# Marking the rows of a bucketed edge sum: three DVE comparisons with a scalar and two ACT operations become one DVE comparison of two tensors

## The reference, cut to what matters

```python
edge_index = jnp.stack([src, dst])
# x: 6250 x 128, edge features: 206250 x 128
row = edge_index[0]                                   # = src, unsorted node numbers
edge_aggr = zeros((n, 128)).at[row].add(edge_features)
combined = concatenate([x, edge_aggr, global_expand], -1) @ W_c + b_c
h = softplus(combined @ W1 + b1)
h = softplus(h @ W2 + b2)
out = layernorm(x + (h @ W3 + b3))
```

## Time and profile before

| | us |
|---|---|
| median of 3 runs | 2045.82 |
| their lowest and highest | 2043.21, 2053.67 |
| the profiled execution's own time | 2045.75 |
| its span, from the first to the last instruction | 2043.8 |

### The profile page before, as it was taken

How to read it: one execution, slowest core, us unless ns; L and a number is a source line. 1 busy time by engine, 2 the same in 40 slices (tenths; PEclk the granted TensorE clock), 3 DMA queues, 4 the chain that set the end, 5 groups by cost and what they waited for, 6 DMA issues and landing times.

```text
span 2043.8 us, 61008 instructions
## 1 busy us (share of the span) xinstructions
PE 1837.2 (90%) x14853; PEld 1709.6 (84%) x14853; DVE 1309.8 (64%) x3881; ACT 1038.7 (51%) x3479; POOL 1170.9 (57%) x1482
## 2 busy tenths in 40 slices
PE   7888988898898989998998889898988999999986
PEld 4788888888888888887888888788888999999973
DVE  7755555555555555555565555555656998899866
ACT  1443443343444444444443444344446888888886
POOL 1656656656655655665665665565564555555535
PEclk9899988898899999899999898999998999999998
DMA  5488666666656665665565556565657999999942
GB/s 139 156 265 277 198 207 207 202 191 211 207 180 173 174 173 166 175 183 165 172 187 173 172 161 184 163 180 161 186 174 222 299 304 300 296 298 305 304 138 61
DMA packets 166150, 413.19 MB, mean 202 GB/s; under 512 B 28533, under 2 KB 43813, under 8 KB 163896
## 3 DMA queue, kind: packets, MB, share of 16 engines
q1 hardware_dynamic: 103824, 234.69, 38.1%
q0 software_dynamic: 54608, 174.58, 27.5%
q10 hardware_dynamic: 7689, 3.60, 1.0%
HBM read 234.52 MB, written 178.23 MB: 202 GB/s over the span
## 4 chain that ended last, share of the span: by engine, by line
PE 77%; issue 8%; DVE 5%; another core or an unknown queue 3%; POOL 1%; ACT 1%; POOLq 1%; DMA 1%; DVEq 0%; ACTq 0%; SPq 0%
PE ps L1228 51%; PE ps L1300 19%; PE ps L1199 2%; PE ps L1186 2%; DVE arena L803 2%; PE ps L1190 1%; DVE hotc L641 1%; DVE arena L875 1%; PE ps L1335 1%; PE ps L1196 1%; DVE slot_f L660 0%; POOL sums L564 0%; DVE picked L652 0%; POOLq L559 0%
## 5 line engine op out<-in xcount | busy, mean ns | idle before, releaser
L1228 PE MATMUL ps<-arena 128*120 128x129 f32 x9084 | 1229.3, 291 | 98.6 <-issue 87.7
L1228 PEld LDWEIGHTS ps<-arena 128*120 128x120 f32 x9084 | 1141.5, 193 | 130.8 <-issue 117.3
L522 POOL DMA_INDIRECT buckets<-arena,index x757 | 778.8, 1029 | 549.2 <-ACT arena L1013 341.3
L803 DVE TENSOR_SCALAR arena<-slot_no,slot_f 128x360 f32<-128x360 f16 x1514 | 549.1, 415 | 601.3 <-PE ps L1228 332.7
L1013 ACT ACTIVATE arena<-ps 120x387 f32<-120x387 f32 x757 | 372.6, 493 | 851.8 <-PE ps L1228 519.5
L1300 PE MATMUL ps<-mark,members 128*128 128x128 f32 x3648 | 412.7, 276 | 9.0 <-ACT mark L1114 7.1
L1300 PEld LDWEIGHTS ps<-mark,members 128*128 128x128 f32 x3648 | 410.5, 192 | 11.2 <-issue 10.4
L847 DVE TENSOR_SCALAR mark<-node_no,members 128x128 f32<-128x128 f16 x1368 | 360.7, 330 | 55.1 <-DMA members<-buckets 45.9
L564 POOL TENSOR_TENSOR sums<-sums,staged 128x128 f32 x456 | 226.4, 496 | 197.5 <-ACT staged L1102 119.5
L968 ACT ACTIVATE reach<-block_no,arena 128x120 f16<-128x120 f16 x806 | 313.4, 391 | 0.7 <-PE ps L1238 0.7
L1108 ACT ACTIVATE apart<-node_no,members 128x128 f32<-128x128 f16 x456 | 181.0, 397 | 34.3 <-DMA members<-buckets 26.6
(11 more groups left out here) (169 smaller groups left out, 634.6 us busy)
## 6 DMA issues: line engine op xcount, KB each, us to landing
members<-buckets SPq DMA_DIRECT2D x456, 258.0 KB, 3.6
arena<-in_feats SPq DMA_DIRECT2D x201, 516.0 KB
buckets<-arena,index POOLq DMA_INDIRECT x757
xn<-in_x ACTq DMA_DIRECT2D x1, 2800.0 KB
arena<-in_xT SPq DMA_DIRECT2D x11, 250.0 KB, 3.9
out_rows<-xn SPq DMA_DIRECT2D x11, 224.0 KB
buckets<-arena,direct_at POOLq DMA_INDIRECT x98
arena<-in_src SPq DMA_DIRECT2D x1, 805.5 KB
```

The lines of the kernel that those rows point to most:

```text
L522: pool.indirect_dma_start(units, bass.IndirectOffsetOnAxis(ap=index[0:SLOTS, s, b:b + 1], axis=0), rows[0:SLOTS, o, :], None).then_inc(sca ...
L803: dve.tensor_scalar(perm[0:TP, b, t, :], slot_no[0:TP, :, :].rearrange("p r b -> p (r b)"), slot_f[0:TP, s, b * TPB + t:b * TPB + t + 1], ...
L1228: mm = pe.matmul(ps[0:SLOTS, MOVED + b, r * ROWF:(r + 1) * ROWF], perm[0:TP, b, t, r * SLOTS:(r + 1) * SLOTS], feat[0:TP, s, b * TPB + t, ...
```

## The change

The four marks of a step are made by one `tensor_tensor` on DVE. Its first input is `node_no` repeated four times, its second the four node numbers of the partition, each repeated 128 times; 512 columns come out. ACT's two operations for the fourth mark, their tile `apart` and the semaphores `apart_made` and `last_marked` are gone. ACT's part of the second phase is the evictions alone, and TensorE waits for `marked` only. Everything else stays as it is.

```diff
             def mark_nodes(s, m, turn):
+
                 dve.wait_ge(members_loaded[m], turn * 16 + 16)
                 wait(dve, summed, s - 3)
-                for r in range(QR - 1):
-                    last = dve.tensor_scalar(mark[:, m % 4, r, :], node_no[:, :],
-                                             members[:, m, r * ROWF + D:(r + 1) * ROWF], None, ALU.is_equal)
-                last.then_inc(marked, 1)
+                ids = members[:, m, :].rearrange("p (r f) -> p r f", f=ROWF)[:, :, D:ROWF]
+                dve.tensor_tensor(mark[:, m % 4, :, :], node_no[:, :].unsqueeze(1).to_broadcast([P, QR, P]),
+                                  ids.to_broadcast([P, QR, P]), ALU.is_equal).then_inc(marked, 1)
...
-            def last_apart(s, m, turn):
-                act.wait_ge(members_loaded[m], turn * 16 + 16)
-                wait(act, last_marked, s - 1)
-                act.activation(apart[:, m % 2, :], node_no[:, :], ACT.Abs, scale=-1.0,
-                               bias=members[:, m, QR * ROWF - 1:QR * ROWF]).then_inc(apart_made, 1)
-
-            def last_mark(s, m):
-                act.wait_ge(apart_made, s + 1)
-                wait(act, summed, s - 3)
-                act.activation(mark[:, m % 4, QR - 1, :], apart[:, m % 2, :], ACT.Relu, scale=-1.0, bias=1.0)\
-                   .then_inc(last_marked, 1)
-
-            def act_step(s, m, turn):
-                ends = isinstance(s, int)
-                if not ends or s + 3 < STEPS:
-                    last_apart(s + 3, (m + 3) % MS, turn + (m + 3) // MS)
-                if not ends or s + 2 < STEPS:
-                    last_mark(s + 2, (m + 2) % MS)
-                evict_sums(s, m)
...
             for m in range(MS):
-                act_step(m, m, 0)
-            with act.Fori(1, STEPS // MS - 1) as i:
+                evict_sums(m, m)
+            with act.Fori(1, STEPS // MS) as i:
                 for m in range(MS):
-                    act_step(i * MS + m, m, i)
-            for m in range(MS):
-                act_step(STEPS - MS + m, m, STEPS // MS - 1)
+                    evict_sums(i * MS + m, m)
...
             def sum_members(s, m):
                 pe.wait_ge(marked, s + 1)
-                pe.wait_ge(last_marked, s + 1)
                 wait(pe, evicted, s + 1 - MS)
```

More of the change, by code:

```diff
@@ L183, in gnn_bucketed_edge_sum_mlp_layernorm @@
         staged = sb("staged", [P, 4, P])
-        apart = sb("apart", [P, 2, P])
         wc = sb("wc", [P, 3, D])
@@ L304, in gnn_bucketed_edge_sum_mlp_layernorm @@
         marked = sem("marked")
-        apart_made = sem("apart_made")
-        last_marked = sem("last_marked")
         summed = sem("summed")
```

## The result

The changed kernel takes 2065.61 us (median of 6 runs) against 2045.59 for the kernel before (6 runs beside them): the ratio is 1.0096, with a 95% interval of 1.0073 to 1.0118, so 15 to 24 us slower. 2059 had been forecast, with 2044 to 2083 as the range. The profiled execution has a span of 2064.0 us against 2043.8.

What follows compares the result with a forecast made beforehand. POOL's instruction stream was taken as the bound, not TensorE. From 2045.75 us, 0.8 gained from evictions and 14.3 lost where DVE and POOL exclude each other gave +13.5, so 2059 us, range 2044 to 2083.

Steps and rivals of the forecast that it cites:

- The bound: Second phase: POOL's instruction stream, 7.26 us a turn, sets the end; TensorE is 0.1 us a turn faster.
- The cost of the comparison: DVE: the one comparison of 512 columns takes 0.69 us, hidden under TensorE's 0.90 us a step.
- Exclusion, and from which point: DVE and POOL: held-off adds end 0.31 us after DVE, held-off comparisons 0.55 after POOL; together 0.86 us a step.
- The sum: POOL's turns in the second phase: 0.25 us lost a turn, 14.3 us over 57 turns, bounds 0 and 44.
- one miss of 0.57 us in three turns: POOL's loop end: an add comes late and waits through a DVE comparison, 0.19 us a turn.
- The term for `b3`: DVE's addition of `b3` after its mark, in 50 of 57 turns, delays POOL: 0.06 us a turn.
- The 0.8 us to be gained from evictions: End of the second phase: POOL waits less because ACT's evictions stand behind nothing, 0.8 us saved, at most 1.1.
- The longest adds: Sign in POOL's adds: mean of 0.55 to 0.65 us instead of 0.496, some above 1.0.
- The wait at the end: Sign at L1321, start of the third phase: TensorE's wait for POOL grows from 2.23 us towards 10.
- Slack: Rival: POOL's slack takes it all and its turn stays 7.26 us; 2045 us, not slower; chance 0.29.
- DVE goes twice before a waiting POOL: Rival: POOL waits through two DVE operations, one more miss of 0.57 us a turn; 2092 us, chance 0.17.
- Full blocking: Rival: DVE and POOL exclude each other for whole instructions, 1.14 us a step; 2151 us, chance 0.02.

Runs made afterwards that it cites:

- the PSUM kernel: Changed kernel with the comparison's node numbers read from PSUM, one input left in SBUF, and sums on four banks instead of eight: 2046.80 us, ratio 1.0007.
- the two kernels with 24 steps: 24 steps instead of 8 in POOL's loop body: in the changed kernel 2049.61 us, ratio 1.0019; in the kernel before 2044.42 us, ratio 0.9987.

## Why the prediction was right

- *The bound.* POOL's instruction stream sets the end, not TensorE's 99.9% busy: shown by the PSUM kernel, where TensorE was faster and the end was not, and by the two kernels with 24 steps, where an edit of POOL's loop alone moved the chain. Reading starts instead of durations was what found it.
- *The cost of the comparison.* 0.69 us forecast; 0.68 to 0.69 where nothing disturbs it, and 0.691 with an input in PSUM. Right.
- *Exclusion, and from which point.* The figure of the earlier trace rows, 0.31 us, holds throughout the changed kernel: all 337 adds of over 0.50 us end 0.30 to 0.33 after an operation of DVE with two inputs in SBUF. The 0.55 us worked out from the earlier trace rows holds too: the 297 comparisons of over 0.72 us that an add held off end 0.55 after it (median; 0.546 to 0.552 for nine in ten). Right.
- *The sum.* 14.3 us for POOL's turns; the chains of two profiles of each kernel differ by 15.3 on average (430.7 against 415.4). That it comes so near is in part luck, for its split was wrong. I had one miss of 0.57 us in three turns, 19 in all, and a slack of 0.12 us from an add of 0.57 that kept its pace. The slack reaches further, to adds of 0.67, so that the longest add of the changed kernel, 0.996, costs 0.33. But there are 99 misses, in 47 of the 57 turns, of 0.17 us in the mean, and only 24 of them are the first add behind a loop's end. Fewer misses of a higher price and more of a lower one gave nearly the same sum. The term for `b3`, 3.4 us, lies inside the 1 to 4 that the runs allow. The 0.8 us to be gained from evictions didn't come: the chain of the PSUM kernel, where they stand behind nothing on ACT either, is 415.0.
- *The rest of the 20 us.* Between the first profiles of both kernels the spans differ by 20.2 us: 16.1 in the chain, 2.2 behind it, where the clock was low in one and not in the other, and 1.9 ahead of it, in the first phase, whose starts scatter by more than that. The forecast had nothing for the last two.
- *The longest adds.* Some above 1.0 were forecast; the longest is 0.996, and 1.014 in the second profile.
- *The wait at the end* was forecast at the first product with `sums`. It came a line earlier, at the product with x, which waits for the evictions: 5.96 + 1.87 us instead of 10.
- *Rivals.* Slack does not take it all: it takes the median add, 0.645, but not the 99 above 0.67. That DVE goes twice before a waiting POOL never happened in the changed kernel: in its trace no add waits through two of DVE's operations, and the longest, 0.996, began when a comparison of 0.69 had just begun (0.69 + 0.31 = 1.00). What the earlier trace rows show is an addition that follows a comparison with a scalar; a comparison of two tensors behind another let POOL in each time. Full blocking would have made 1.14 us a step; the chain has 431.0 / 456 = 0.95.

## What to carry to other kernels

An engine with 57% busy time can be the bound: take the distance between the starts of its instructions and compare it with that of the engine that looks full, before crediting anything to the latter. When an operation gets a second tensor input in SBUF, look at what POOL does beside it, add up how long both hold the other off in one step, and if it comes near the step's length, try one input in PSUM: here that cost banks but no time, and took the whole loss back. Cutting the operation into two shorter pieces gained nothing here, because their sum no longer fitted.

## What the runs showed of the hardware that I had not expected

TensorE's granted clock fell during the wait at the end of the second phase, and stayed low for a while even under load. A stretch of the changed kernel:

```profile
1985.70:1995.90 10.20, 6.42 (x11) 3.44 (x12) 0.48 (x1) 2.54 (x7) 2.72 (x6) 0.50 0.00 0
```

TensorE had made nothing since 1981.66. Its clock was still at 1.00, the 2.4 GHz level, up to 1985.6, and at 0.50, the 1.2 GHz level, from 1985.7 to 1995.9, although it had work again from 1987.62 on. Where it was kept busy with spare products the clock stayed at 1.00. The length of the wait alone doesn't say whether the clock falls. In the first profile of the kernel before it stayed at 1.00 through waits of 0.46 and 2.2 us; in the second, with waits of 0.46 and 1.3 us, the ten us behind the chain have 0.83. In the PSUM kernel, where the waits were 2.56 and 1.87 us, they have 0.81. A mean between 0.5 and 1 is a stretch partly at the 1.2 and partly at the 2.4 GHz level.
